# A Mamba block on one core: the slot programs are reordered and half of the clamped sums go back to GpSimd

## The reference

```python
h = layernorm(x)
xi, z = split(h @ in_proj.T)                  # 1024 channels each
xc = silu(causal_conv1d(xi, 4 taps) + conv_b)
xp = xc @ x_proj.T                            # 1 + 16 + 16 columns: dt, B, C
delta = softplus(xp[..., 0:1] * dt_w + dt_b)
# in chunks of 128 rows, for each of the 16 states s (A_s < 0):
log_A_cum = cumsum(log(max(exp(delta * A_s), 1e-10)))
A_cum     = exp(min(log_A_cum, 80))
wcum      = cumsum(delta * B_s * xc / max(shifted A_cum, 1e-10))
h_chunk   = A_cum * wcum / max(A_bar, 1e-10) + h_before * A_cum
y         = sum_s C_s * h_chunk + D * xc
x1  = x + (y * silu(z)) @ out_proj.T
out = x1 + int8_matmul(layernorm(x1), rhs)    # rows and columns scaled by their absolute maximum
```

## Time and profile before

| | |
|---|---|
| time, median of 3 runs | 6438.85 us (6435.35 to 6446.21) |
| the profiled execution's own time | 6439.85 us |
| its span, first to last instruction | 6438.1 us |
| TensorE busy | 5799.8 us (90%) |
| VectorE busy | 5095.2 us (79%) |
| ScalarE busy | 4907.5 us (76%) |
| GpSimd busy | 2985.4 us (46%) |
| mean granted TensorE clock | 0.962 |

### The profile page before, as it was taken

One profiled execution on the slowest core, in us unless ns is written; L12 is line 12 of the kernel. 1 busy time (PEld: TensorE's weight loads), 2 busy tenths in 40 slices (PEclk: granted clock), 3 DMA queues, 4 the chain that ended last, 5 costly groups with the idle time before them and its releaser, 6 DMA issues. The chain is left out here.

```text
span 6438.1 us, 76746 instructions
## 1 busy us (share of the span) xinstructions
PE 5799.8 (90%) x16152; PEld 2688.6 (42%) x16152; DVE 5095.2 (79%) x6545; ACT 4907.5 (76%) x5642; POOL 2985.4 (46%) x1627
## 2 busy tenths in 40 slices
PE   5899899999898998999999999989999899998997
PEld 2444444444444444444444444444444444444443
DVE  4778787788787887887878878878778778788786
ACT  4777777777777877777777777777777777777776
POOL 2445444454444444544544444444445444444453
PEclk9999999999999999999999999999999999999998
DMA  1121121121211211212112112111121121121110
GB/s 62 11 17 18 11 18 14 14 18 12 16 15 13 18 15 13 18 12 16 18 13 16 15 13 18 14 14 18 13 16 17 13 16 15 13 18 13 16 16 11
DMA packets 157920, 104.46 MB, mean 16 GB/s; under 512 B 121008, under 2 KB 121008, under 8 KB 157488
## 3 DMA queue, kind: packets, MB, share of 16 engines
q1 hardware_dynamic: 157488, 100.71, 17.2%
HBM read 42.63 MB, written 16.78 MB: 9 GB/s over the span
## 5 line engine op out<-in xcount | busy, mean ns | idle before, releaser
L487 POOL TENSOR_TENSOR acc<-acc,term 128x1024 f32<-128x1024 f32 x512 | 1430.1, 2793 | 3044.5 <-DVE term L1355 3044.5
L987 PE MATMUL cum<-step,tri_before 128*128 128x512 f32 x4096 | 2023.3, 618 | 70.0 <-POOL step L475 67.9
L997 PE MATMUL state<-sources,tri_upto 128*128 128x512 f32 x4096 | 1950.9, 599 | 49.7 <-DVE term L1347 48.5
L713 ACT ACTIVATE decay<-cum,neg_a 128x1024 f32<-128x1024 f32 x1024 | 1133.3, 1107 | 945.2 <-PE cum L987 936.7
L1347 DVE SCALAR_TENSOR_TENSOR term<-state,crow,decay 128x1024 f32<-128x1024 f32 x1024 | 1310.5, 1280 | 656.9 <-PE state L997 544.4
L475 POOL TENSOR_SCALAR step<-delta,limit 128x1024 f32<-128x1024 f32 x1024 | 1412.1, 1388 | 294.2 <-PE cum L987 292.9
L1329 DVE SCALAR_TENSOR_TENSOR sources<-cum,brow,dx 128x1024 f32<-128x1024 f32 x1024 | 1303.7, 1273 | 12.4 <-ACT cum L728 12.4
L722 ACT ACTIVATE room<-total,curve,neg_a 128x1024 f32<-128x1024 f32 x1024 | 1263.3, 1234 | 12.0
L987 PEld LDWEIGHTS cum<-step,tri_before 128*128 128x128 f32 x4096 | 792.3, 198 | 1044.8 <-issue 899.8
L892 PE MATMUL fbank<-win,xnT 128*128 128x512 f32 x2048 | 1030.7, 628 | 137.2 <-ACT xiT L582 109.5
L728 ACT ACTIVATE cum<-room,curve 128x1024 f32<-128x1024 f32 x1024 | 1142.9, 1116 | 14.9
(11 more groups left out here) (126 smaller groups left out, 4406.5 us busy)
## 6 DMA issues: line engine op xcount, KB each, us to landing
hfirst<-hrows SPq DMA_DIRECT2D x496, 64.0 KB, 3.9
xt<-in_x SPq DMA_DIRECT2D x64, 256.0 KB, 2.6
hrows<-term SPq DMA_DIRECT2D x1024, 4.0 KB, 1.7
xres<-in_x SPq DMA_DIRECT2D x64, 256.0 KB, 2.7
out_x<-xres SPq DMA_DIRECT2D x64, 256.0 KB, 2.1
gate_last<-gate SPq DMA_DIRECT2D x512, 0.5 KB, 2.0
win<-in_w_in SPq DMA_DIRECT2D x2, 2048.0 KB, 11.0
hrows<-hrows SPq DMA_DIRECT2D x64, 64.0 KB, 2.3
```

The costliest lines, as they stand in the source:

```text
L487: nc.gpsimd.tensor_tensor(sums, sums, term[term_at(s - 1)][:, :], ALU.add).then_inc(added, 1)
L713: nc.scalar.activation(decay[s % 4][:, :], cum[s % 2][:, :], ACT.Exp, scale=neg_a[:, s:s + 1]).then_inc(decay_ready, 1)
L987: last = nc.tensor.matmul(cum[s % 2][:, cols], tri_before[:, :], step[s % 2][:, cols], start=True, stop=True)
L997: last = nc.tensor.matmul(state[:, cols], tri_upto[:, :], source[s % 2][:, cols], start=True, stop=True)
```

## The change

- GpSimd gets the clamped sum (`limit_sum`) of slots 0, 2, 5, 6, 9, 10, 12 and 13 (`ROOM_POOL`); ScalarE keeps the other eight. The growth of these slots reads the clamp with a scale of its own.
- The taps are worked off in two halves of the channels. VectorE has them in slots 4, 5 and 6 (before 5, 6 and 7). The first moments of the layernorm go from slot 4 to slot 7 on VectorE.
- The silu into `xcT`, with the silu of the gate, goes from slot 8 to slot 7 on ScalarE; `proj` from slot 9 to 8 on TensorE, the transposes of xc to slots 9 and 10.
- On ScalarE the emptying of xc0 stands ahead of the growth in slot 9 and that of xc1 behind the growth of slot 10. abs stands in slot 9; exp and square stand at the head of slots 10 and 11; ln goes to slot 11; `decay_once` to slot 15.
- `total1` and the transpose of `xn` use `ebank`, so that total0 and total1, and ct and xn, have a bank each. New waits keep `ebank` free: total1 waits for x2 of the tile before, the transposes of q for both.
- Parts 1 to 3 of the output projection stand in slots 9, 10 and 11 (before 8, 10 and 11).

```diff
+ROOM_POOL = (0, 2, 5, 6, 9, 10, 12, 13)
+            def limit_sum(t, s):
+                if s == ROOM_POOL[0]:
+                    pool.wait_ge(front_act, at(FRONT_ACT, t, "total1"))
+                user, old = before(t, s, 1)
+                if user is not None:
+                    pool.wait_ge(growth_ready, slot_at(user, old))
+                stand(pool)
+                nc.gpsimd.tensor_scalar(room[:, :], total[:, :], limit[:, s:s + 1], 0.0,
+                                        ALU.min, ALU.max).then_inc(limited, 1)
@@ GpSimd, body
                         limit_step(nxt, s + 3 - NS)
+                    if s + 2 < NS and s + 2 in ROOM_POOL:
+                        limit_sum(t, s + 2)
+                    if more and s + 2 >= NS and s + 2 - NS in ROOM_POOL:
+                        limit_sum(nxt, s + 2 - NS)
@@ ScalarE, growths
-                act.wait_ge(room_ready, slot_at(t, s))
-                nc.scalar.activation(cum[s % 2][:, :], room[:, :], ACT.Exp, bias=ln_top, scale=-1.0).then_inc(growth_ready, 1)
+                if s in ROOM_POOL:
+                    act.wait_ge(limited, room_at(t, s))
+                    nc.scalar.activation(cum[s % 2][:, :], room[:, :], ACT.Exp, scale=pos_a[:, s:s + 1]).then_inc(growth_ready, 1)
@@ ScalarE, body
-                    if s == 10 and more:
-                        front_abs(nxt)
+                        if s == 10:
+                            front_exp(nxt)
+                        if s == 11:
+                            front_square(nxt)
+                        if s == 15:
+                            decay_once(nxt)
                         if s == 9:
-                            front_proj(nxt)
+                            front_xc(nxt, 0)
                         if s == 11:
-                            front_xc(nxt, 1)
-                            front_square(nxt)
+                            front_log(nxt)
+                        if s == 7:
+                            front_xcT(nxt)
                         if s == 8:
-                            front_xcT(nxt)
-                    if s == 8:
+                            front_proj(nxt)
+                    if s == 7:
                         gate_silu(t)
+                        if s == 9:
+                            front_abs(nxt)
                         if s == 10:
-                            front_xc(nxt, 0)
-                            front_log(nxt)
+                            front_xc(nxt, 1)
@@ TensorE, body
-                        if s == 9:
+                        if s == 8:
                             front_proj(nxt)
-                        if s == 10:
-                            front_xc(nxt, 0)
+                        if s in (9, 10):
+                            front_xc(nxt, s - 9)
                         if s == 13:
                             front_total(nxt, 0)
+                            front_total(nxt, 1)
-                    if prev is not None and s in (10, 11):
+                    if prev is not None and s in (9, 10, 11):
                     states(t, s)
-                    if more:
-                        if s == 10:
-                            front_xc(nxt, 1)
-                        if s == 13:
-                            front_total(nxt, 1)
@@ VectorE, body
-                        if s == 5:
-                            front_tap0(nxt)
-                        if s in (6, 7):
-                            front_tap(nxt, s - 5)
+                        if s == 4:
+                            front_tap(nxt, 0, 0)
+                            front_tap(nxt, 1, 0)
+                        if s == 5:
+                            front_tap(nxt, 2, 0)
+                            front_tap(nxt, 0, 1)
+                        if s == 6:
+                            front_tap(nxt, 1, 1)
+                            front_tap(nxt, 2, 1)
+                            front_halo_out(nxt)
```

More of the change, by code:

```diff
@@ L50 @@
 NORM_PE = ("xnT",)
-FRONT_DVE = ("halo_in", "tap0", "tap1", "tap2", "halo_out", "b_rows", "c_rows", "c_last", "dt_lin", "under", "poly",
+FRONT_DVE = ("halo_in", "tap0a", "tap1a", "tap2a", "tap0b", "tap1b", "tap2b", "halo_out", "b_rows", "c_rows", "c_last", "dt_lin", "under", "poly",
              "log1p", "delta", "dx")
-FRONT_ACT = ("xi0", "xi1", "xiT0", "tap3a", "xiT1", "tap3b", "z0", "xcT", "proj", "abs", "exp", "over", "xc0",
-             "ln", "xc1", "square", "z1", "total0", "total1", "ct")
+FRONT_ACT = ("xi0", "xi1", "xiT0", "tap3a", "xiT1", "tap3b", "z0", "xcT", "proj", "xc0", "abs", "exp", "over", "xc1",
+             "square", "ln", "z1", "total0", "total1", "ct")
 FRONT_PE = ("xi0", "xi1", "xiT0", "xiT1", "z0", "proj", "xc0", "xc1", "z1", "total0", "total1", "ct")
@@ L101, in term_at, with room_at @@
     return 2 if slot % 2 else slot // 2 % 2
+def room_at(tile, slot):
+    same = [s for s in range(NS) if (s in ROOM_POOL) == (slot in ROOM_POOL)]
+    return tile.n * len(same) + same.index(slot) + 1
 def ring_at(tile, slot):
@@ L525, in start @@
                     limit_step(t, s)
+                for s in range(2):
+                    if s in ROOM_POOL:
+                        limit_sum(t, s)
             def body(t, more, more2):
@@ L678, in front_total @@
                 if prev is not None:
[L679 to L680 removed]
+                    act.wait_ge(growth_ready, slot_at(prev, NS - 1))
+                evacuate(t, f"total{h}", total[:, h * HALF:(h + 1) * HALF], (fbank, ebank)[h][:, :])
             def decay_once(t):
@@ L715, in rooms @@
             def rooms(t, s):
-                if s == 0:
+                if s == min(x for x in range(NS) if x not in ROOM_POOL):
                     act.wait_ge(front_act, at(FRONT_ACT, t, "total1"))
@@ L765, in start @@
                 for s in range(2):
-                    rooms(t, s)
+                    if s not in ROOM_POOL:
+                        rooms(t, s)
                     decays(t, s)
@@ L776, in body @@
                         end_q(prev2)
-                    if s == 10 and more:
-                        front_abs(nxt)
+                    if more:
+                        if s == 10:
[4 more added lines that the diff above has]
+                            decay_once(nxt)
                     if more or s + 2 < NS:
-                        rooms(ahead, slot)
+                        if slot not in ROOM_POOL:
+                            rooms(ahead, slot)
                         decays(ahead, slot)
@@ L918, in front_total @@
             def front_total(t, h):
+                earlier = t.shift(-2)
                 pe.wait_ge(front_dve, at(FRONT_DVE, t, "delta"))
-                front_free(t, f"total{h}")
-                nc.tensor.matmul(fbank[:, :], tri_before[:, :], delta[t.parity][:, h * HALF:(h + 1) * HALF],
+                if h == 0:
+                    front_free(t, "total0")
+                elif earlier is not None:
+                    pe.wait_ge(end_dve, at(END_DVE, earlier, "x2"))
+                nc.tensor.matmul((fbank, ebank)[h][:, :], tri_before[:, :], delta[t.parity][:, h * HALF:(h + 1) * HALF],
                                  start=True, stop=True).then_inc(front_pe, 1)
@@ L964, in end_attn, with end_qT @@
                     last.then_inc(end_pe, 1)
-            def end_qT(t):
+            def end_qT(t, turned_in=None, summed_in=None):
+                if turned_in is not None:
+                    pe.wait_ge(norm_act, at(NORM_ACT, turned_in, "xnT"))
+                if summed_in is not None:
+                    pe.wait_ge(front_act, at(FRONT_ACT, summed_in, "total1"))
                 pe.wait_ge(end_act, at(END_ACT, t, "q"))
@@ L1062, in body @@
                         if s == 0:
-                            end_qT(prev2)
+                            end_qT(prev2, nxt if more else None, t)
                         if s == 1:
@@ L1380, in start @@
                 front_halo(t)
-                front_tap0(t)
-                front_tap(t, 1)
-                front_tap(t, 2)
+                for h in range(2):
+                    for tap in range(3):
+                        front_tap(t, tap, h)
+                front_halo_out(t)
                 front_rows(t)
```

67 lines of the change are left out of this document (35 added, 32 removed).

## The result

The changed kernel takes 6330.24 us (median of 4 runs, 6328.38 to 6333.05), against 6438.4 us before in the same comparison. The ratio is 0.9831 with a 95% interval of [0.9814, 0.9848]: 1.7% faster. This is clear of the noise, though under 2%. I had forecast 5920 us, with a range from 5780 to 6200 us. The direction was right and the size wrong: of some 520 us, 108 came.

The account below looks back on a forecast made before the run. TensorE was taken as the bound: a floor of 85.5 us per tile plus collisions of 1.5, 0.5 and 0.3, the loop's turn 1.65 and 1.05 gave 90.5 against 98.76, so 5920 us; eight-in-ten range 5780 to 6200 us.

Parts of the forecast that it names:

- The 9.4 us of slots 10 and 11: TensorE's loss per tile around xc0, xc1 and z1, of 13.3 us lost in all; forecast to go.
- xc0, xc1, proj: On their new places each ScalarE emptying comes ahead of the TensorE step that needs it; the 9.4 us go.
- the softplus chain: abs to delta: delta ends at about 33 us, TensorE wants it at 35.3; holds nobody, some 2 us to spare.
- the two banks: total1 no longer waits for total0's emptying, nor xn's transpose for ct's; the latter is 0.9 us per tile.
- the contention: VectorE with two SBUF inputs and GpSimd shut each other out; eight added clamps priced at 0 to 9.0 us per tile.
- three collisions of 1.5, 0.5 and 0.3 us: Per tile: slot 8's step meets taps, 1.5; slot 9's clamp behind a late add, 0.5; next tile's first step, 0.3.
- One of my signs of being wrong: Clock falling in each tile, proj waiting over 2 us for the silu, or VectorE busy above 85 us per tile.
- My bound for the contention: Eight added GpSimd clamps cost from 0 to 8 × 1.12 = 9.0 us per tile; value taken near the low end.
- VectorE becoming the bound through the lock: Slower rival: VectorE waits out clamps in slots 12 to 15, 18 us against 11.4 gained, about 6850 us; chance 0.04.
- my rivals of 6170 and 6850 us: Stall moved to slots 8 to 10, 6170 us, chance 0.24; VectorE bound through GpSimd's lock, about 6850 us, chance 0.04.
- a lump for what I could not place: 1.05 us per tile added for latencies left out of the walk and collisions that could not be placed.
- the rival to which I gave 0.24: Stall moves to slots 8 to 10: slot 9's clamp 3 us late, clock falls, 94.5 us per tile, 6170 us.

Follow-up runs that it names:

- the two versions with mended runs: Changed kernel with whole taps in slots 5 to 7, 6224.48 us; changed kernel with the pair behind the taps in slots 4 and 6, 6224.14 us.

## Why the prediction was wrong

**What bounds the kernel: right.** The 9.4 us of slots 10 and 11 were there to be had, and they are gone from the trace of the changed kernel. The parts on xc0, xc1, proj, the softplus chain and the two banks hold in each point that shows: of the waits for `xiT` 5.2 us in all are left, and none for ct.

**The step that failed** is the contention, where I wrote "I take a value near the low end" and placed three collisions of 1.5, 0.5 and 0.3 us. The taps by halves in slots 4 to 6 were given no price at all: I read from the earlier trace rows that a run of taps keeps GpSimd out and costs GpSimd alone, and passed over the run of slot 5, where a tap of 1.2 us was in my own rows. In the changed kernel it is the other way about in two of three runs. Slot 4 has no small instruction ahead of its taps, so the add goes in at once; in slot 6 flag stands ahead, and the add goes in at the wait between the dependent halves. Taps cost VectorE 473 us more, 7.4 us per tile, and TensorE's wait for the term 426.1 - 48.5 = 378 us, 5.9 us per tile, with a fall of the clock behind it. The missing 97.1 - 90.5 = 6.6 us per tile are of this size. One of my signs of being wrong showed: VectorE is busy for 5610.6 / 64 = 87.7 us per tile, over the 85 that I had named, and the mean clock is 0.971, not above 0.98.

That this is a cause and not only a fit is shown by the halves alone in the kernel before, 5.4% slower, and by the pair between the halves, which takes the changed kernel from 0.983 to 0.937 of the time before. But it isn't the only one. Four kernels, with the add released ahead of the taps or behind them and with clamps on GpSimd or not, make a table:

| | eight clamps on GpSimd | all on ScalarE |
|---|---|---|
| pair ahead of the taps (runs broken) | 6330.24 us | 6195.06 us |
| pair behind the taps | 6224.14 us | 5862.58 us |

Mending the runs alone gives 106 us and taking the clamps back alone 135 us, but both together 468 us. Once the runs are whole the late clamp of slot 9 holds TensorE instead, and while they are broken TensorE waits only 3.1 us for the silu. Both are collisions of VectorE and GpSimd that my sum left out or placed at 0.5 us.

My bound for the contention, 0 to 9.0 us per tile, did hold the loss, but by luck: I priced it for the clamps, not for the taps, and took its low end. To VectorE becoming the bound through the lock I gave 0.04. The time came out between my rivals of 6170 and 6850 us, and neither of them names the broken runs.

**The terms that were right in size.** With the pair between the halves, TensorE waits 1.5 us for the step of slot 8, though in half of the tiles only, 0.85 us for the step that starts a tile, and 41.5 / 64 = 0.65 us for the silu (1.5, 0.3 and 0.5 forecast). In the changed kernel itself the 0.85 us are the only regular wait for a step, 54.8 us in 63 waits, and there is no wait for the silu to speak of (3.1 us in all). With the pair behind the taps and all sums on ScalarE, the period is (5751.8 - 102.8) / 63 = 89.7 us, where I had 90.5, and the time 5862.6 us, where I had 5920. With seven clamps on GpSimd it is 5870.5 us. The forecast was that of a kernel in which neither the add goes into the taps nor the clamp of slot 9 is late; since 1.05 us of it was a lump for what I could not place, part of the agreement is luck.

**The clamps.** I gave them no cost but the 0.5 us of slot 9. In the changed kernel they cost 135 us, and in the version with the pair behind the taps one of them, slot 9's, costs about 350 us, through growth, silu and proj and the fall of the clock behind them. This is the rival to which I gave 0.24, with 6170 us. Its mechanism is seen only in the two versions with mended runs, which measured 6224 us both; the changed kernel's time is not its doing.

**The rule of the Trainium skill.** I cited the Trainium skill (SBUF — State Buffer, "Who interferes with whom") for an exclusive lock held for the whole instruction. The open runs agree: taps of 0.34 us took 2.1 us more behind an add and 0.9 us more behind a clamp. What I read into it was wrong: the lock is held per instruction, so an open run of eight short ones is eight chances to lose it, each at the price of GpSimd's long one. The closed runs don't agree with "whoever starts first": in slot 6 of the kernel before, an add that began 0.08 us after the first tap waited out seven taps that started after it.

## What to carry to other kernels

Count the short VectorE instructions with two SBUF inputs that meet long GpSimd work, and price each at up to one whole GpSimd instruction: a run may stay closed in one slot and be open in the next, so the cheap case in the old trace is no bound for the new one. Read every run of the old trace, not only the cheap ones: a mean of 447 ns beside one of 336 for the same instruction was the sign here. Release GpSimd's long work (here by the pair) after such a run or where VectorE reads PSUM, and keep a dependent neighbour out of the run. Then look at what is queued behind the work that became later: one clamp in a chain of three engines cost more than the other seven together. Mend such faults together before judging either, since each alone gave 106 and 135 us of 468.

## What the runs showed of the hardware

- GpSimd and VectorE took turns once GpSimd was in. In slot 6 of the changed kernel an add and three clamps (two steps and a room) were served while the last four taps waited, so that taps spaced by 0.26 us stood 1.12 us apart.
- One VectorE instruction on a single element with a pointer scalar closed the run behind it to GpSimd, whatever its output type. In the kernel before, the runs of slots 6 and 7 both stand behind such an instruction and both kept GpSimd out; that it closed the second run too was not tried by itself. Copies of one column on 128 partitions closed nothing. Whether it takes the single partition, and why, is open.
- A wait between two dependent taps moved the next start from 0.26 to 0.37 us, and this 0.1 us was enough for an add of 2.4 us to go in.
